# Message layer of a graph network: sixteen additions on TensorE in one piece of sixteen tiles or two pieces of eight

## The reference

```python
x = layernorm(x + L0(edge_index, x))           # sum over edges of x[src] / sqrt(deg[src] * deg[dst])
x = layernorm(x + L1(x, edge_index, sh, feat)) # the message layer
```

```python
h = relu(edge_feat @ W1 + b1); w = (h @ W2 + b2).reshape(e, 4, 8, 8)
m0 = ALPHA * (einsum('ei,eio->eo', s[src]*sh0, w_000) + C110 * einsum('eim,em,eio->eo', v[src], sh1, w_110))
m1 = ALPHA * (einsum('ei,em,eio->eom', s[src], sh1, w_011) + einsum('eim,eio->eom', v[src]*sh0, w_101))
out = concat(segment_sum(m0, dst), segment_sum(m1, dst)) + linear terms of x
```

## Time and profile before

| what | value |
|---|---|
| median of three runs | 5100.83 us (5097.14 to 5117.32) |
| span of the profiled execution | 5099.5 us |
| TensorE busy, matmuls / weight loads | 2903.2 us (57%) / 2114.7 us (41%) |
| VectorE busy | 2791.7 us (55%) |
| GpSimd busy | 2381.5 us (47%) |
| ScalarE busy | 1398.2 us (27%) |

### The profile page before, as it was taken

The page is one execution under the profiler, slowest core; times in us unless marked ns, Lnnn a source line. Parts: engine busy times, 40 slices in busy tenths (PEclk is TensorE's granted clock), DMA queues, the critical chain, the costliest instruction groups (busy, mean ns, idle before and its releaser), DMA issues.

```text
span 5099.5 us, 54067 instructions
## 1 busy us (share of the span) xinstructions
PE 2903.2 (57%) x20030; PEld 2114.7 (41%) x20030; DVE 2791.7 (55%) x4344; ACT 1398.2 (27%) x1651; POOL 2381.5 (47%) x2475
## 2 busy tenths in 40 slices
PE   5566666666666664545545465455554555555555
PEld 3344444445444453333433343343333333333344
DVE  7444544445444534555655566556655655665566
ACT  3454555455545551111111111111111111111111
POOL 2444444453444335554455545545554554555453
PEclk7787878787878877677776677767767767777777
DMA  2000000000000010000000001100010110011011
GB/s 50 9 8 9 9 8 8 9 9 8 8 9 9 10 22 17 19 19 18 20 19 19 19 17 21 19 18 19 19 21 15 22 19 17 19 19 22 17 19 26
DMA packets 187965, 84.72 MB, mean 17 GB/s; under 512 B 131337, under 2 KB 174153, under 8 KB 187721
## 3 DMA queue, kind: packets, MB, share of 16 engines
q0 software_dynamic: 78336, 40.26, 5.4%
q1 hardware_dynamic: 109385, 41.08, 3.6%
HBM read 76.34 MB, written 4.81 MB: 16 GB/s over the span
## 4 chain that ended last, share of the span: by engine, by line
PE 30%; DVE 25%; issue 24%; another core or an unknown queue 14%; ACT 4%; DVEq 1%; DMA 1%; POOL 0%; SPq 0%; POOLq 0%; ACTq 0%
DVE stage L1404 10%; PE ps L767 9%; PE ps L881 8%; PE ps L724 6%; DVE prod_all L1394 5%; PE ps L782 5%; ACT room L572 4%; DVE prod_all L1388 3%; DVE oh L1108 2%; PE ps L873 1%; PE ps L755 1%; DVE prod_all L1220 1%; DVE stage L1413 1%; DVE sumT_all L1127 1%
## 5 line engine op out<-in xcount | busy, mean ns | idle before, releaser
L522 POOL DMA_INDIRECT xg<-x_table,idx x1664 | 1569.6, 943 | 1637.9 <-DVE stage L1378 1045.9
L881 PE MATMUL ps<-w2t,hT 128*128 128x256 f32 x3328 | 1037.4, 451 | 617.5 <-issue 403.6
L522 POOL DMA_INDIRECT xg<-scaled_x_table,idx x784 | 803.4, 1025 | 1007.8 <-issue 587.8
L881 PEld LDWEIGHTS ps<-w2t,hT 128*128 128x128 f32 x3328 | 736.8, 226 | 1019.0 <-issue 781.5
L572 ACT ACTIVATE room<-ps 128x1089 bf16<-128x1089 f32 x800 | 908.5, 1188 | 853.6 <-remote 495.6
L1388 DVE TENSOR_TENSOR prod_all<-ps,stage 128x768 f32<-128x768 f32 x416 | 397.7, 956 | 1245.4 <-remote 660.7
L767 PE MATMUL ps<-prod_all,lane 128*128 128x363 bf16 x2640 | 636.8, 355 | 577.5 <-issue 181.6
L724 PE MATMUL ps<-oh,stage 128*64 128x76 f32 x3328 | 378.0, 275 | 796.9 <-issue 561.7
L627 ACT ACTIVATE hT<-ps,b 64x512 f32<-64x512 f32 x416 | 284.1, 683 | 1764.0 <-remote 739.0
L1404 DVE TENSOR_REDUCE stage<-prod_all 128x192 f32<-128x1536 f32 x416 | 723.6, 1741 | 0.0
L724 PEld LDWEIGHTS ps<-oh,stage 128*64 128x64 f32 x3328 | 329.4, 175 | 819.7 <-issue 551.4
(11 more groups left out here) (141 smaller groups left out, 1312.5 us busy)
## 6 DMA issues: line engine op xcount, KB each, us to landing
efT<-in_efT SPq DMA_DIRECT2D x104, 256.0 KB
xg<-x_table,idx POOLq DMA_INDIRECT x1664
xg<-scaled_x_table,idx POOLq DMA_INDIRECT x784
sh<-in_sh SPq DMA_DIRECT2D x104, 32.0 KB
idx<-in_src SPq DMA_DIRECT2D x104, 8.0 KB
idx<-in_src SPq DMA_DIRECT2D x98, 4.0 KB
scaled_x_table<-room SPq DMA_DIRECT2D x2, 784.0 KB, 7.6
x_table<-x_sb SPq DMA_DIRECT2D x7, 224.0 KB, 4.3
```

The source lines that it names most:

```text
L522: pool.indirect_dma_start(rows[k][:, t, :], None, table, bass.IndirectOffsetOnAxis(ap=idx[k][:, t:t + 1], axis=0),).then_inc(s_g[layer][k] ...
L881: mm = pe.matmul(ps_w[j % 2][:, t, :], hT[j % 2][:, t * P:(t + 1) * P], w2t[:].rearrange("p c o i -> p (c o i)"), start=True, stop=True)
```

## The change

`window_sums` gets an argument `tiles`: the tiles it adds. Its waits stand ahead of the first tile, its signal behind the last. In `chunk`, on the path that runs, tiles 0 to 7 of chunk n - 1 are added at j = 2 behind the weights of group 1, tiles 8 to 15 at j = 3 behind the weights of group 2. What follows in the queue is the next chunk's hidden pair and the weights of group 3. The six chunks that finish rows, the first chunk and what follows the last are as they were; so are the first layer and the other path.

```diff
@@ -707,23 +707,25 @@
                 if groups_out[0]:
                     pe.wait_ge(s_ld[0], groups_out[0])
 
-            def window_sums(layer, rows, n):
+            def window_sums(layer, rows, n, tiles=range(TPC)):
 
                 k = n % 2
-                if layer == 0:
-                    pe.wait_ge(s_g[0][k], 16 * TPC * (n // 2 + 1))
-                else:
-                    pe.wait_ge(s_msg, 2 * n + 2)
-                pe.wait_ge(s_oh[layer], n + 1)
-                if layer == 0:
-                    wait_sums_bank()
-                    chunks_in[0] += 1
-                elif n >= 1:
-                    pe.wait_ge(s_acc[1], SPC * n)
-                for t in range(TPC):
+                if tiles[0] == 0:
+                    if layer == 0:
+                        pe.wait_ge(s_g[0][k], 16 * TPC * (n // 2 + 1))
+                    else:
+                        pe.wait_ge(s_msg, 2 * n + 2)
+                    pe.wait_ge(s_oh[layer], n + 1)
+                    if layer == 0:
+                        wait_sums_bank()
+                        chunks_in[0] += 1
+                    elif n >= 1:
+                        pe.wait_ge(s_acc[1], SPC * n)
+                for t in tiles:
                     mm = pe.matmul(ps_sum[layer][:, t // TPS, :], rows[:, t, :], oh[layer][k][:, t, :],
                                    start=(t % TPS == 0), stop=(t % TPS == TPS - 1))
-                mm.then_inc(s_sum[layer], 1)
+                if tiles[-1] == TPC - 1:
+                    mm.then_inc(s_sum[layer], 1)
 
             def wide_sums(layer, rows, n, landed):
 
@@ -886,7 +888,7 @@
 
                 return msg[n % 2][:, :, M0:M1]
 
-            def chunk(n, k, edges, at, sums, done=None):
+            def chunk(n, k, edges, at, sums, done=None, pieces=1):
 
                 g = GPC * n
                 for j in range(GPC):
@@ -896,14 +898,18 @@
                         weights(g + j - 1, (j - 1) % 2, at == 0 and j < 3)
                     if done is not None and j == 0:
                         sums_to_rows(1, done, n - 1, 0)
-                    if j == (2 if done is None else 3) and at >= 1:
+                    if done is None and pieces == 2:
+                        if j >= 2 and at >= 1:
+                            sums(n - 1, range((j - 2) * TPC // 2, (j - 1) * TPC // 2))
+                    elif j == (2 if done is None else 3) and at >= 1:
                         if done is not None:
                             pe.wait_ge(s_ld[1], done + 1)
                         sums(n - 1)
 
             with pe.If(all_near == 1):
                 for n in range(CHUNKS):
-                    chunk(n, n % 2, 32 * (n // 2) + 32, n, lambda m: window_sums(1, message_rows(m), m), rows_at.get(n))
+                    chunk(n, n % 2, 32 * (n // 2) + 32, n,
+                          lambda m, tiles=range(TPC): window_sums(1, message_rows(m), m, tiles), rows_at.get(n), 2)
                 weights(GPC * CHUNKS - 1, 1, False)
                 window_sums(1, message_rows(CHUNKS - 1), CHUNKS - 1)
                 sums_to_rows(1, NG - 1, CHUNKS, 0)
```

## The result

The changed kernel takes **4953.6 us** (median, 4931.2 to 4965.8 over four runs) against 5100.3 us before: a ratio of 0.9701, 95% interval 0.9678 to 0.9723. The forecast of 5197 us had the wrong sign; the time lies inside the range, near the price of rival A (4900 us). Some gathers run alone and some in pairs, a mixture that none of the forecast's cases had.

What follows compares the result with a forecast made beforehand. Bound: TensorE's answers to VectorE come late while GpSimd's gathers run in the message layer. Lone gathers cost +1.0 us a chunk, x 96 = +96; 5099.5 + 96 + 1.3 = 5197 us, range 4900 to 5380.

Steps and rivals of the forecast that it cites:

- rival A: Message layer: gathers run alone but group 3 is answered earlier, about 17.8 us after the gather's start; about 4900 us, chance 0.28.
- What bounds the kernel: Message layer: while indirect DMAs run, TensorE's answers come late after a certain number of instructions; chunks start every 30.0 us.
- The plain TensorE time: Message layer: 16 matmul-load pairs take about 1.7 us; neither the first piece nor the additions' wait adds time.
- The count: Group 3's weights become the 34th matmul after the gather's start instead of the 18th, answered at 20.9 us instead of 9.0.
- the crawl: TensorE's slow stretch while gathers run: 6 matmuls and 6 loads in 14 us, 2.3 us a pair.
- the hold's end: Time until which a lone gather keeps TensorE's answers late: 22.8 us after its start, taken as upper bound for group 3.
- the break-even: Group 3's answer 19.9 us after the gather's start, which with 10.1 us more gives today's 30.0 us a chunk.
- What follows: From group 3's answer to the next gather 10.1 us; each chunk becomes a lone gather of 31.0 us, +1.0 a chunk.
- rival C: Gathers stay in pairs, up to 0.7 + 1.7 us more a pair: 5101 to 5216 us, chance 0.20.
- The clock: Group 2's weights may run at half clock more often after a shorter burst: 0 to 0.55 us a chunk, taken as zero.

Runs made afterwards that it cites:

- twelve and four: The changed kernel with its sixteen tiles divided as twelve at j = 2 and four at j = 3: 5146.6 us, 1.0088 of the kernel before.

## Why the prediction was wrong

**What bounds the kernel** held. Late answers of TensorE while gathers run set the time: halving the gathers removed the remote wait, and keeping the gathers apart gave 8 to 11%.

**The plain TensorE time** held as far as it can be seen: 16 pairs of the second piece took 1.27 us in the chunk shown (1.7 forecast), well inside the 16.9 us to the answer.

**The count** had its mechanism right and its size wrong, and here the sign was lost. The step that failed is "Two pairs at 2.3 us earlier is 4.7 us less", with its "mean is G + 20.9". It took the 36th matmul, of a pair's second chunk, as the nearest row and the crawl of TensorE's own records, 14/6 us, as the price of a matmul-load pair. Measured, the 34th after a lone gather's start is answered at G + 16.9 in the median, and a matmul-load pair costs 0.7 us between the 34th and the 42nd. The rows taken are those of joined gathers: at G + 20 the second gather starts, and the latest answer, 3330.81, comes 22.8 us after the second gather's start at 3307.98, the end of that gather's hold; in the earliest VectorE has no idle time, so the answer may have been there sooner. They say little of a lone gather. A row of one was not at hand in the kernel before, where no ordinary gather is alone; but both ends were, a prompt 18th and the hold's end at 22.8 for a lone gather. 20.9 stood one us above the break-even of 19.9 that the prediction itself named, while the rows bounded the answer only between 10.7 and 22.8: with bounds so wide the faster side deserved more than the 0.28 of A.

**What follows** held in its parts: the next gather starts 10.0 us after the answer (10.1 forecast), and a lone chunk is the answer plus that, 26.9 us. It failed in "each chunk becomes a lone gather": 21 pairs stayed, their group 3 being answered at G + 8.6 to 11.6 with the same 34th matmul. Had all become lone at 26.6 us, the gain would have been (30.0 - 26.6) x 96, about 326 us, by estimate. These remaining pairs are rival C's, and cost what C said: without chunks that finish rows 61.8 us in the mean against 60.0, 1.8 more a pair where C allowed up to 2.4.

**The clock.** The prediction set it at nothing, as the one row it showed was already cold (3.75 us). That row was not typical. At the starts of lone gathers and pairs in ordinary chunks, weights of group 2 took 3.7 us or more in 6 of 48 before (median 3.1) and in 61 of 77 in the changed kernel (median 3.75), though the layer's granted clock rose from 0.71 to 0.73. One of each, from the kernel before and the changed one:

```profile
3941.68 1.97 PE L881 MATMUL ps<-w2t,hT 128*128 128x256 f32 x8 [1.96 <-DVE prod_all L1394]
```

```profile
2149.11 3.75 PE L883 MATMUL ps<-w2t,hT 128*128 128x256 f32 x8 [3.52 <-DVE prod_all L1400]
```

VectorE's wait before the products of group 2 rose from 0.10 to 0.55 us in the median. So with 16 pairs ahead of G group 2 was more often cold, and in the rows shown TensorE stood idle for 3.52 us before it in place of 1.96. The Trainium skill ("TensorE: Matmul & The Clock Gate", section "Why this matters for your kernels") asks for no long idle gaps between bursts of matmuls. The trace agrees with it as far as it goes: 3.75 us behind the longer gap, 1.97 behind the shorter one. The length of the piece does not decide it alone (cold in 10 of 48 with twelve tiles ahead of G, in 66 of 87 with four, in 38 of 91 with none). In the lone chunk shown that costs no time: group 3's weights are recorded as over by G + 9.1 in spite of it, and VectorE waits for their signal until G + 16.9. What it costs where the answer is prompt was not measured by itself.

## What to carry to other kernels

When an engine's answers come late only while another engine's transfers run, ask first when those transfers start, and then how much work stands ahead of each signal: one wait on GpSimd, which delays a gather on purpose until the held signal is there, brought almost four times what moving the sums did (578 us against 147). Where a change of pattern is forecast, the sign hangs on its break-even, here an answer at G + 19.9; if the estimate is within its own error of that point, give both sides like weight. A single row taken as the usual case, as with the clock here, wants a count of how many rows are like it. A mean near which nothing lies, like 29.0 us a chunk made of 26.6 and of pairs of 63.8, wants its two kinds counted before it is explained.

## What the runs showed of the hardware

Beside a gather of 16 indirect DMAs, about 26 matmul-load pairs of TensorE since the gather's start are answered promptly (G + 9.2 in the median of twelve and four). The 34th is answered at G + 16.9, and each further one 0.7 us later up to the 42nd, as medians of lone gathers; the 50th comes at G + 22.6, 3.9 us after the gather's last DMA starts. The matmuls are recorded as over long before that, 7.7 us in the lone gather shown. With gathers of 8 DMAs spaced 18.6 us apart no remote wait before the products was left. In the changed kernel a pause of 3.5 us between gathers of 16 was enough for the next to be answered like any other, and one of 2.6 to 2.8 us was not in seven cases of eight. That a kernel gets 11% faster by starting each gather later in its chunk was not expected.
